# Local-attention stack on one core: spreading copies of one slot in eight on VectorE, the input's split two slots later, the first gate copy behind the squares of Q, and a rotary sum as one addition

## The chip, the cores and the metric

One NeuronCore of a Trainium2 chip runs the whole program. The metric is the device time of one execution in microseconds (us). Engines: TensorE (PE in the profile, its weight loads PEld), VectorE (DVE), ScalarE (ACT), GpSimd (POOL), and the DMA queues, which SyncE (SP) fills. Each engine works its own list of instructions in order; they meet only through semaphores.

## The reference

`x` is 8 x 256 x 128. After one layer norm without gains, two branches are computed and added to `x`: a causal attention (16 heads of 64, keys and values through a latent of 128), and a stack of 6 layers. A layer is

```python
def attn_layer(x, Wqkv, qs, ksc, Wo):
    q, k, v = split(x @ Wqkv)                     # 16 heads of 64
    q, k = l2norm(q) * qs, l2norm(k) * ksc
    q = q * cos * scale + rotate_half(q) * sin * scale
    k = k * cos / scale + rotate_half(k) * sin / scale
    return local_attention(q, k, v) @ Wo          # windows of 32 and the window before
def ffn_layer(x, g, bln, W1, b1, W2, b2):
    xn = layernorm(x) * g + bln
    a, gate = split(xn @ W1 + b1)                 # 341 each
    return a * gelu(gate) @ W2 + b2
for i in range(6):
    x = attn_layer(shift_tokens(x), ...) + x
    x = ffn_layer(shift_tokens(x), ...) + x
```

`rotate_half` puts minus the second half of a head's 64 features before the first half. All is float32.

## The kernel before, in words

**Stages.** The layer norm and the causal attention come first (to about 340 us). Then a stream of 192 slots does the six layers. A *unit* is one batch element of one layer (48 of them), a *group* is 4 of its 16 heads, and slot `s` is the step in which group `s` has its window scores computed. At the same time slot `s` works on other groups at other stages: it projects K, Q and V of group `s+4` (`keys`, `queries`, `values`, lines 1020 to 1040, three matmuls to a product of float32r halves), norms group `s+3` (L975, L703, L706), weighs the values of group `s-1` (L1016), projects the output of group `s-2` (L943), and does the MLP of two units, spread over slots 13 to 20 of a pair (`mlp_slot(s, k)` is true where `s` is `k` modulo 8). The pattern repeats every 8 slots. Below, **slot kind k** is a slot whose number is k modulo 8. In kinds 5, 6, 7 the gate's three products are done (L1077, copied out by L730), in kinds 1, 2, 3 the three of the other half (L1091, multiplied with the gate by `hidden_out`, L1373), in kind 4 the down projection (L1099). In kind 2 and kind 6 the centring matmul of the layer norm (L1113) follows, in the same PSUM bank `B_M` as the MLP, and in kinds 3 and 7 its variance (L1121).

**Order.** It is written out by hand: every engine has a function `slot(s)` that lists what it does in the slot.

- TensorE (lines 1042 to 1121): turn the probabilities of `s-1` (L1004), scores of `s` (L994), K, output projection, norms (L975), values (L1016), the MLP's product, Q, V, and last the centring (L1113) or variance (L1121). L1016 waits for `spread_ready`. L994 waits for `mask_laid`; only in kind 1 does TensorE lay the mask itself (L985). L1113 waits in kind 2 for `hid_ready` of the slot's own `hidden_out`, since it writes the bank which that reads.
- VectorE (lines 1393 to 1429): residual of the MLP, `shift_windows` (L1309, L1311), rotation of K (L1330, L1331), `weigh_down` (L1316 to L1321), the clamp of the norms (L1410), `residual` in kinds 1 and 5, `split_input` in kinds 0 and 4 (L1335 casts a unit's input to float32r, L1337 subtracts to get the rest), `hidden_out`, and last the rotation of Q, which waits for `q_square`.
- ScalarE (lines 682 to 745): `spread_out(s-1)` (L638 twice: the turned probabilities go from PSUM bank `B_T` to `spread`, two halves of 64 partitions), the exponentials (L699), logarithm and exponential of the norms (L703, L706), output copy (L670), squares of K (L629), gate copy (L730) in kinds 5, 6, 7, `lay_masks(s+1)` (L663), squares of Q (L629 again), the copy of the values (L569). `lay_masks` waits for `weights_ready` (L1321). At the end of kind 0 comes the **gelu session**: a table load (L674), two gelus (L676, L680), and at the start of kind 1, behind `spread_out`, the load back (L694).
- GpSimd (lines 442 to 470): the rotary sum of K (`rotated`, L439, two additions of 128x256), its norming (L432, released by L1410), the sum of squares (L459), norming of Q, the rotary sum of Q. In four slots of each of the five changes of layer it also splits the next weights (L420, L427). `rotate` on VectorE waits for the rotary sum before (`k_summed`, `q_summed`).
- SyncE: the copies of z and of shifted values for the windows, and the weights.

Of the kernel before, what the change touches and what calls it, by code (L numbers as in the profile page):

```python
# [11 lines left out]
ALU = mybir.AluOpType  # L12
ACT = mybir.ActivationFunctionType
# [4 lines left out]
NB, T = 8, 256  # L18
# [3 lines left out]
G, HG = 4, 4  # L22
# [3 lines left out]
WIN = 32  # L26
LN_EXP = "natural_log_exp_and_others"
INNER = P * 4 * 2 // 3
CW = [P, P, INNER - 2 * P]
# [11 lines left out]
KEYS = 2 * WIN  # L41
TILES = P // WIN

UNITS = DEPTH * NB
GROUPS = UNITS * G
LAYER = NB * G
# [55 lines left out]
def build(nc, x, w_kv_down, w_kv_up, w_q, w_out, Wqkv, q_scale, k_scale, Wo, ln_g, ln_b, W1, b1, W2, b2, const, out):  # L102
    with ExitStack() as ctx:
# [101 lines left out]
        def after(eng, name, value):  # L205

            if not (isinstance(value, int) and value <= 0):
                eng.wait_ge(S[name], value)
# [38 lines left out]
        def active(s, first, last):  # L247

            return first <= s < last

        def mlp_slot(s, first):

            return s % (2 * G) == first % (2 * G) and first <= s < first + 2 * G * MLPS
# [152 lines left out]
        def _(pool):  # L406
# [27 lines left out]
            def rotated(m, parity, idx, prod, mark):  # L434

                pool.wait_ge(S[prod], m + 1)
                after(pool, "zn_ready", m - 1)
                for half in range(2):
                    a = pool.tensor_tensor(z_raw[:, parity, idx, half, :], rot_u[:, idx, half, :], rot_v[:, idx, 1 - half, :], ALU.add)  # L439
                a.then_inc(S[mark], 1)  # L440

            def slot(s):
                one, two = active(s, -4, GROUPS - 4), active(s, -3, GROUPS - 3)
# [76 lines left out]
        def _(act):  # L520
# [105 lines left out]
            def squares(m, done, src, idx, mark):  # L626
                act.wait_ge(S[done], m + 1)
                after(act, "sums_ready", m)
                act.activation(sq[:, idx, :, :], src[:, :].rearrange("p (a t) -> p a t", a=2), ACT.Square).then_inc(S[mark], 1)  # L629
# [35 lines left out]
            def output_out(n):  # L665
# [3 lines left out]
                after(act, "lwo_done", n + 1 - G)  # L669
                act.activation(yt[:, 2 * og:2 * og + 2, :], B_T.rearrange("p (c t) -> p c t", c=2), ACT.Copy).then_inc(S["lyt_ready"], 1)  # L670

            def gelus(p):

                act.preload_act_table(ACT.Gelu)  # L674
                act.wait_ge(S["gate_ready"], 3 * p + 3)
                act.activation(gate[:, 0:2, :], gate[:, 0:2, :], ACT.Gelu).then_inc(S["gelu_done"], 1)  # L676
# [5 lines left out]
            def slot(s):  # L682
                g = s % G
                one, two = active(s, -4, GROUPS - 4), active(s, -3, GROUPS - 3)
                three, four = active(s, 0, GROUPS), active(s, 1, GROUPS + 1)
                normed = g == 0 and active(s, 2 * G, 2 * G + GROUPS)
                if two and s >= 0 and not mlp_slot(s, 17):
                    values_out(s + 3)
                if s == 1:
                    act.wait_ge(S["spread_zero"], 2)  # L690
                if four:
                    spread_out(s - 1)
                if mlp_slot(s, 17):
                    act.preload_act_table_set(LN_EXP)  # L694
                if normed:
                    deviations((s - 8) // G, B_M)
                if three:
                    act.wait_ge(S["shifted"], s + 1)
                    act.activation(both, both, ACT.Exp).then_inc(S["raised"], 1)  # L699
                if two:  # L700
                    m = s + 3
                    act.wait_ge(S["n_done"], m + 1)
                    act.activation(ln_n(m), B_N[:, :].rearrange("p (a t) -> p a t", a=2), ACT.Ln, bias=tiny[:, 0:1], scale=LNS).then_inc(S["ln_done"], 1)  # L703
                    act.wait_ge(S["ln_done"], m + 1)
                    after(act, "zn_ready", m)
                    act.activation(rinv(m), ln_n(m), ACT.Exp, scale=-0.5).then_inc(S["rinv_ready"], 1)  # L706
                if four:
                    output_out(s - 1)
                if one:
                    squares(s + 4, "k_prod", B_K, 1, "k_square")  # L710
                l = layer_begun(s, LAYER - 5)
                if l:
                    rotary_scales(l)
                    rotary_tables(l, 1)
                l = layer_begun(s, LAYER - 4)
                if l:
                    act.wait_ge(S["q_prod"], LAYER * l)
                    rotary_tables(l, 0)
                if g == 3 and active(s, 7, 7 + GROUPS):
                    xc_squares((s - 7) // G)  # L720
                if normed and s % (2 * G) == G:
                    gained((s - 8) // G)
                if s % (2 * G) == 1 and active(s, 9, 9 + GROUPS):
                    gained((s - 9) // G)
                for c in range(3):
                    if mlp_slot(s, 13 + c):
                        p = (s - 13 - c) // (2 * G)
                        act.wait_ge(S["gate_done"], 3 * p + c + 1)
                        after(act, "hid_ready", 3 * p + c - 2)
                        act.activation(gate[0:CW[c], c, :], B_M[0:CW[c], :], ACT.Identity, bias=gate_bias[0:CW[c], c:c + 1]).then_inc(S["gate_ready"], 1)  # L730
                if active(s, 0, GROUPS - 1) and lays_mask(s + 1):
                    lay_masks(s + 1)
                if one:
                    squares(s + 4, "lq_done", B_Q, 0, "q_square")
                if mlp_slot(s, 16):
                    if active(s + 1, -3, GROUPS - 3):
                        values_out(s + 4)
                    gelus((s - 16) // (2 * G))
                    last_gelus((s - 16) // (2 * G))
                l = layer_begun(s, LAYER + 6)  # L740
                if l:
                    gains(l)
                l = layer_begun(s, LAYER + 10)
                if l:
                    gate_biases(l)
# [470 lines left out]
        def _(dve):  # L1216
# [86 lines left out]
            def by_block(a):  # L1303
                return a[:, :, :].rearrange("p (a b) x -> p a (b x)", a=2)

            def shift_windows(n):

                dve.wait_ge(S["scores_done"], n + 1)
                dve.tensor_reduce(by_block(nm), both, AX_X, ALU.max, negate=True).then_inc(S["top_ready"], 1)  # L1309
                dve.wait_ge(S["top_ready"], n + 1)  # L1310
                dve.tensor_tensor(both, both, by_block(nm).unsqueeze(3).broadcast_to([P, 2, 4, KEYS]), ALU.add).then_inc(S["shifted"], 1)  # L1311
# [81 lines left out]
            def slot(s):  # L1393
                g = s % G
                one, two, three = active(s, -4, GROUPS - 4), active(s, -3, GROUPS - 3), active(s, 0, GROUPS)
                if mlp_slot(s, 21):
                    mlp_residual((s - 21) // (2 * G), B_M)
                if g == 3 and active(s, 7, 7 + GROUPS):
                    centred_out((s - 7) // G)
                if three:  # L1400
                    shift_windows(s)
                if one:
                    rotate(s + 4, 1, B_K, "lk_done", "k_summed", "k_prod")
                if g == 0 and active(s, 8, 8 + GROUPS):
                    normed_out((s - 8) // G)
                if three:
                    weigh_down(s)
                if two:
                    dve.wait_ge(S["rinv_ready"], s + 4)
                    dve.tensor_scalar(rinv(s + 3), rinv(s + 3), 1e12 / ROOT, None, ALU.min).then_inc(S["bound_ready"], 1)  # L1410
                if s == 0:
                    dve.wait_ge(S["wo_done"], NB + 1)
                    dve.tensor_copy(attn[:, NB - 1, :], B_Y[:, 0:T]).then_inc(S["res_done"], 1)
                if g == 1 and active(s, 5, 5 + GROUPS):
                    residual((s - 5) // G)
                if g == 0 and active(s, -4, GROUPS - 8):
                    unit = (s + 8) // G
                    after(dve, "lv_done", G * (unit - 1))
                    after(dve, "mlp_res", (s + 8 - LAYER) // (2 * G) + 1)
                    split_input(unit, (s + 8) // G % NB, (s + 8) // G % 2)  # L1420
                for c in range(3):
                    if mlp_slot(s, 17 + c):
                        p = (s - 17 - c) // (2 * G)
                        hidden_out(p, c, B_M, 2 * p + (2 if c == 2 else 1))
                if one:
                    rotate(s + 4, 0, B_Q, "q_square", "q_summed", "q_prod")
                l = layer_begun(s, LAYER + 15)
                if l:
                    out_biases(l)
# [93 lines left out]
```

## Time and profile before

| | |
|---|---|
| median of 3 runs | 1923.13 us (1921.1 to 1923.8) |
| profiled execution | 1922.0 us, its span 1920.2 us |
| TensorE, VectorE, ScalarE, GpSimd busy | 94%, 82%, 77%, 72% of the span |
| granted TensorE clock | 0.999 of full speed |
| one turn of 8 slots in the stream | 64.75 us (the one from 988.86 us on); 68.99 us where a layer changes |

The profile is of one execution. A duration in a timeline is that of one instruction from start to end; instructions of one engine overlap by about 0.1 us, so the distance of two starts is shorter. An idle time in brackets stands with the engine's next instruction and names whose signal ended it.

### The profile page before, as it was taken

Reading aid. Unit: us, or ns where it says so; the run is one execution under the profiler, and the core shown is the slowest. Engines: PE = TensorE matmul, PEld = TensorE weight load, DVE = VectorE, ACT = ScalarE, POOL = GpSimd, SP = SyncE. Lnnn points to the kernel's source line nnn. Section 1 sums busy time; section 2 is a strip of 40 time slices with the busy share of each in tenths; the row PEclk is TensorE's granted clock in tenths of the full one; section 3 lists DMA queues with packets and bytes.
Section 4 is the critical chain, followed back from the end, with each engine's and each line's share of the span. In section 5 each row is a group of like instructions: output and inputs, shape, how many; then the busy total and the mean of one; then the engine's idle time right before and its main releaser. Section 6 shows DMA issues by size and latency. Waiting matters only on the chain.

```text
span 1920.2 us, 68296 instructions
## 1 busy us (share of the span) xinstructions
PE 1813.2 (94%) x26763; PEld 1373.4 (72%) x26763; DVE 1572.1 (82%) x3052; ACT 1480.1 (77%) x3020; POOL 1374.0 (72%) x1455
## 2 busy tenths in 40 slices
PE   6999998999989999999999899999999998999997
PEld 4777765777767777777777677777777776777774
DVE  5776777888888888888888888888888888888886
ACT  5766665688778878887887788788878887887885
POOL 3010024898898787897888987878978889888880
PEclk9999999999999999999999999999999999999999
DMA  4000001344434334333334343343333443433332
GB/s 133 1 1 0 0 0 37 98 107 107 129 88 108 101 99 129 91 96 102 101 101 127 86 110 99 99 134 90 96 100 99 105 128 83 112 96 100 100 98 71
DMA packets 193540, 171.03 MB, mean 89 GB/s; under 512 B 32304, under 2 KB 190168, under 8 KB 193240
## 3 DMA queue, kind: packets, MB, share of 16 engines
q1 hardware_dynamic: 193240, 166.89, 33.1%
q8 instruction: 206, 3.38, 0.8%
q14 instruction: 94, 0.77, 0.1%
HBM read 21.01 MB, written 1.05 MB: 11 GB/s over the span
## 4 chain that ended last, share of the span: by engine, by line
PE 59%; ACT 18%; DVE 11%; issue 9%; SPq 1%; POOL 1%; DMA 0%; ACTq 0%; DVEq 0%; POOLq 0%
PE bank L975 6%; PE bank L1016 6%; PE bank L943 5%; PE pair_bank L994 5%; PE bank L1025 4%; ACT probs L703 3%; ACT sq L629 3%; PE bank L1027 3%; PE bank L1026 3%; PE bank L1077 2%; PE bank L1099 2%; ACT yt L670 2%; PE bank L1004 2%; PE bank L860 2%; PE bank L1091 2%
## 5 line engine op out<-in xcount | busy, mean ns | idle before, releaser
L439 POOL TENSOR_TENSOR z_raw<-rot_u,rot_v 128x256 f32<-128x256 f32 x768 | 552.7, 744 | 70.4 <-DVE rot_v L1331 67.8
L432 POOL TENSOR_TENSOR z_norm<-probs_t,z_raw 128x512 f32<-128x512 f32 x376 | 480.8, 1279 | 119.6 <-DVE probs_t L1410 117.4
L1330 DVE TENSOR_TENSOR rot_u<-bank,tabs 128x512 f32<-128x512 f32 x384 | 263.0, 685 | 160.0 <-ACT sq L629 159.8
L1025 PE MATMUL bank<-x_high,w_high 128*128 128x256 f32 x768 | 301.7, 393 | 0.2 <-issue 0.2
L459 POOL TENSOR_TENSOR sqs<-sq 128x512 f32<-128x512 f32 x192 | 250.5, 1305 | 71.0 <-issue 70.9
L1016 PEld LDWEIGHTS bank<-probs_t,v_late 128*64 128x64 f32 x3072 | 157.6, 137 | 160.1 <-issue 160.1
L1331 DVE TENSOR_TENSOR rot_v<-bank,tabs 128x512 f32<-128x512 f32 x384 | 261.3, 680 | 0.0
L699 ACT ACTIVATE pair_bank<-pair_bank 128x512 f32<-128x512 f32 x192 | 111.7, 582 | 190.7 <-DVE pair_bank L1311 189.7
L638 ACT ACTIVATE probs_t<-bank 64x512 f32<-64x512 f32 x384 | 226.5, 590 | 24.6 <-PE bank L1004 22.1
L629 ACT ACTIVATE sq<-bank 128x512 f32<-128x512 f32 x384 | 224.9, 594 | 26.6 <-PE bank L1027 20.4
L1027 PE MATMUL bank<-x_low,w_high 128*128 128x256 f32 x768 | 216.4, 282 | 0.0
L1026 PE MATMUL bank<-x_high,w_low 128*128 128x256 f32 x768 | 216.3, 282 | 0.0
L1016 PE MATMUL bank<-probs_t,v_late 128*64 128x64 f32 x3072 | 198.8, 228 | 15.3 <-ACT probs_t L638 15.3
L975 PE MATMUL bank<-sqs,consts 128*128 128x512 f32 x384 | 197.5, 596 | 6.0 <-POOL sqs L459 5.8
L943 PE MATMUL bank<-yt,wo 128*128 128x256 f32 x768 | 197.8, 380 | 0.0
L994 PE MATMUL pair_bank<-zqk 64*32 64x64 f32 (+1 forms) x12288 | 164.9, 221 | 30.2 <-ACT pair_bank L663 29.6
L1016 PE MATMUL bank<-probs_t,v_sb 128*64 128x64 f32 x3072 | 190.2, 222 | 0.0
L1025 PEld LDWEIGHTS bank<-x_high,w_high 128*128 128x128 f32 x768 | 144.8, 189 | 58.5 <-issue 39.0
L994 PEld LDWEIGHTS pair_bank<-zqk 64*32 64x32 f32 x12288 | 134.9, 105 | 65.8 <-issue 64.2
L1026 PEld LDWEIGHTS bank<-x_high,w_low 128*128 128x128 f32 x768 | 145.5, 189 | 36.9 <-issue 36.9
L703 ACT ACTIVATE probs<-bank,tiny 128x512 f32<-128x512 f32 x188 | 129.2, 687 | 45.4 <-PE bank L975 43.1
L1016 PEld LDWEIGHTS bank<-probs_t,v_sb 128*64 128x64 f32 x3072 | 158.6, 138 | 0.0
(184 smaller groups left out, 4525.5 us busy)
## 6 DMA issues: line engine op xcount, KB each, us to landing
zqk<-z_norm SPq DMA_DIRECT2D x1536, 64.0 KB, 2.1
v_late<-v_sb SPq DMA_DIRECT2D x192, 192.0 KB, 2.6
w_qkv<-in_L_ffn_Wqkv SPq DMA_DIRECT2D x18, 512.0 KB
v_late<-v_sb SPq DMA_DIRECT2D x192, 32.0 KB, 3.0
wo<-in_L_ffn_Wo SPq DMA_DIRECT2D x24, 128.0 KB, 2.4
w<-in_L_ffn_W SPq DMA_DIRECT2D x12, 170.5 KB, 2.6
z_norm<-in_L_attn_x SPq DMA_DIRECT2D x4, 256.0 KB, 5.1
w_qkv<-in_L_attn_w_kv_up SPq DMA_DIRECT2D x4, 256.0 KB, 4.5
```

The costliest lines, as they stand in the source:

```text
L432: return pool.tensor_tensor(z_norm[:, parity, idx, :, :], rinv(m)[:, idx, :].unsqueeze(1).broadcast_to([P, 2, T]), z_raw[:, parity, idx, : ...
L439: a = pool.tensor_tensor(z_raw[:, parity, idx, half, :], rot_u[:, idx, half, :], rot_v[:, idx, 1 - half, :], ALU.add)
L629: act.activation(sq[:, idx, :, :], src[:, :].rearrange("p (a t) -> p a t", a=2), ACT.Square).then_inc(S[mark], 1)
L943: mm = pe.matmul(B_X[:, 0:T], wo[:, c, :], yt[:, c, :], start=(c == 0), stop=(c == HD // P - 1))
L975: pe.matmul(B_N[:, :], con("blk"), sqs[:, :, :].rearrange("p a t -> p (a t)"), start=True, stop=True).then_inc(S["n_done"], 1)
L994: mm = pe.matmul(bank[a][WIN * tile:WIN * tile + WIN, at + skip:at + KEYS], zqk[rows, g, 0, pair, WIN * j:WIN * j + WIN], zqk[rows, g, 1, ...
L1016: mm = pe.matmul(y[:, t, tile % 2, :, :], (v_sb if tile % 2 else v_late)[:, odd, t, f], spread[:, h, tile, :], start=True, stop=True, tile ...
L1025: pe.matmul(dst, w_high[:, j, cols], x_high[:, odd, :], start=True, stop=False)
L1026: pe.matmul(dst, w_low[:, j, cols], x_high[:, odd, :], start=False, stop=False)
L1027: mm = pe.matmul(dst, w_high[:, j, cols], x_low[:, odd, :], start=False, stop=True)
L1330: dve.tensor_tensor(rot_u[:, idx, :, :], src, tabs[:, 2 * idx, :, :], ALU.mult)
L1331: dve.tensor_tensor(rot_v[:, idx, :, :], src, tabs[:, 2 * idx + 1, :, :], ALU.mult).then_inc(S[mark], 1)
```

## The change

1. In the 22 slots of kind 1 from slot 17 on, `spread_out(s-1)` is VectorE's first step, as two copies, and no longer ScalarE's: there the load back (L694) follows the gelus.
2. `split_input` of a unit stands in kinds 2 and 6, two slots later, with the same waits; in VectorE's list it stays ahead of `hidden_out` and of the rotation of Q.
3. The gate copy of kind 5 (c = 0) stands behind `lay_masks` and the squares of Q; those of kinds 6 and 7 stay.
4. `rotated` on GpSimd is one addition of 128x512 with `rot_v` read in reversed order of its halves, in place of two of 128x256.

```diff
@@ GpSimd, rotated @@
-                for half in range(2):
-                    a = pool.tensor_tensor(z_raw[:, parity, idx, half, :], rot_u[:, idx, half, :], rot_v[:, idx, 1 - half, :], ALU.add)
-                a.then_inc(S[mark], 1)
+                pool.tensor_tensor(z_raw[:, parity, idx, :, :], rot_u[:, idx, :, :], rot_v[:, idx, ::-1, :], ALU.add).then_inc(S[mark], 1)
@@ ScalarE, slot @@
-                if four:
+                if four and not mlp_slot(s, 17):
                     spread_out(s - 1)
                 if mlp_slot(s, 17):
                     act.preload_act_table_set(LN_EXP)
...
-                for c in range(3):
+                for c in (1, 2):
                     if mlp_slot(s, 13 + c):
...
+                        gate_out((s - 13 - c) // (2 * G), c)
                 if active(s, 0, GROUPS - 1) and lays_mask(s + 1):
                     lay_masks(s + 1)
                 if one:
                     squares(s + 4, "lq_done", B_Q, 0, "q_square")
+                if mlp_slot(s, 13):
+                    gate_out((s - 13) // (2 * G), 0)
@@ VectorE @@
+            def spread_out(n):
+
+                dve.wait_ge(S["turned"], n + 1)
+                after(dve, "lpv_done", n)
+                tiles = B_T.rearrange("p (h s c) -> p h s c", h=HG, s=TILES)
+                for x in range(2):
+                    rows = slice(KEYS * x, KEYS * x + KEYS)
+                    a = dve.tensor_copy(spread[rows, :, :, WIN * x:WIN * x + WIN], tiles[rows, :, :, :])
+                a.then_inc(S["spread_ready"], 1)
@@ VectorE, slot @@
+                if mlp_slot(s, 17) and active(s, 1, GROUPS + 1):
+                    spread_out(s - 1)
                 if mlp_slot(s, 21):
                     mlp_residual((s - 21) // (2 * G), B_M)
...
-                if g == 0 and active(s, -4, GROUPS - 8):
-                    unit = (s + 8) // G
+                if g == 2 and active(s, -2, GROUPS - 6):
+                    unit = (s + 6) // G
                     after(dve, "lv_done", G * (unit - 1))
-                    after(dve, "mlp_res", (s + 8 - LAYER) // (2 * G) + 1)
-                    split_input(unit, (s + 8) // G % NB, (s + 8) // G % 2)
+                    after(dve, "mlp_res", (s + 6 - LAYER) // (2 * G) + 1)
+                    split_input(unit, unit % NB, unit % 2)
                 for c in range(3):
                     if mlp_slot(s, 17 + c):
```

`gate_out` on ScalarE holds the three lines of the gate copy that stood in the loop (wait for `gate_done`, wait for `hid_ready`, the activation of L730).

## Rows read from the trace of the kernel before

**Rows 1.** Waits: engine and line waiting, releaser: us in total, times, longest
```profile
PE pair_bank L994 <- ACT pair_bank L663: 29.6, 46, 0.8
...
PE bank L1016 <- ACT probs_t L638: 15.3, 23, 0.7
...
PE bank L975 <- POOL sqs L459: 5.8, 7, 1.0
```

**Rows 2.** ScalarE's timeline, gelu session (kinds 0 and 1): start, us, instruction
```profile
991.12 0.61 ACT L680 ACTIVATE gate<-gate 85x512 f32<-85x512 f32 x1
991.64 1.18 ACT L638 ACTIVATE probs_t<-bank 64x512 f32<-64x512 f32 x2
992.83 1.28 ACT L694 ACT_TABLE_LOAD   x1
...
997.43 0.60 ACT L663 ACTIVATE pair_bank<-mask_local_b 128x512 f32<-128x512 bf16 x1
```

**Rows 3.** TensorE's timeline, kinds 1 and 2
```profile
992.96 0.34 PE L1016 MATMUL bank<-probs_t,v_late 128*64 128x64 f32 x4 [0.66 <-ACT probs_t L638]
...
998.18 0.84 PE L994 MATMUL pair_bank<-zqk 64*32 64x32 f32 x64 [0.84 <-ACT pair_bank L663]
...
1005.09 0.67 PE L1113 MATMUL bank<-xs,consts 128*128 128x256 f32 x2
```

**Rows 4.** VectorE's timeline, kinds 1 and 2
```profile
990.91 0.68 DVE L1309 TENSOR_REDUCE nm<-pair_bank 128x8 f32<-128x512 f32 x1
...
998.58 0.69 DVE L1330 TENSOR_TENSOR rot_u<-bank,tabs 128x512 f32<-128x512 f32 x1 [0.30 <-ACT sq L629]
...
1004.20 0.74 DVE L1373 SCALAR_TENSOR_TENSOR hid<-bank,out_bias,gate 128x512 f32<-128x512 f32 x1
```

**Rows 5.** VectorE's timeline, end of kind 0, a turn later
```profile
1052.68 0.29 DVE L1335 CAST x_high<-xs 128x256 fp32r<-128x256 f32 x1
1053.01 1.40 DVE L1337 TENSOR_TENSOR x_low<-xs,x_high 128x256 fp32r<-128x256 f32 x1
1054.33 0.68 DVE L1330 TENSOR_TENSOR rot_u<-bank,tabs 128x512 f32<-128x512 f32 x1
```

**Rows 6.** ScalarE (squares of K and Q) and GpSimd beside rows 5
```profile
1052.02 1.07 ACT L629 ACTIVATE sq<-bank 128x512 f32<-128x512 f32 x2
...
1052.85 1.28 POOL L432 TENSOR_TENSOR z_norm<-probs_t,z_raw 128x512 f32<-128x512 f32 x1 [0.69 <-DVE probs_t L1410]
```

**Rows 7.** Lines L1337 and L1299: ns min/median/max, first and last start
```profile
L1337 DVE TENSOR_TENSOR x_low<-xs,x_high x48: 426/1394/1403, 284.6 to 1809.9; 128x256 fp32r<-128x256 f32 x48
...
L1299 DVE COPY zqk<-bank x32: 678/681/692, 17.2 to 280.5; 128x512 f32<-128x512 f32 x32
```

**Rows 8.** ScalarE's timeline, kind 5
```profile
1029.69 0.69 ACT L730 ACTIVATE gate<-bank,gate_bias 128x512 f32<-128x512 f32 x1
1030.26 0.61 ACT L663 ACTIVATE pair_bank<-mask_local_b 128x512 f32<-128x512 bf16 x1
```

**Rows 9.** VectorE and TensorE beside rows 8
```profile
1029.09 0.69 DVE L1321 TENSOR_TENSOR probs<-pair_bank,rrec 128x512 f32<-128x512 f32 x1 [0.23 <-DVE rrec L1318]
...
1031.02 0.84 PE L994 MATMUL pair_bank<-zqk 64*32 64x32 f32 x64 [0.46 <-ACT pair_bank L663]
```

**Rows 10.** A change of layer, kind 2 on VectorE and kind 6 on TensorE
```profile
541.84 1.67 DVE L1410 TENSOR_SCALAR probs_t<-probs_t 128x512 f32<-128x512 f32 x1
...
572.06 0.84 PE L994 MATMUL pair_bank<-zqk 64*32 64x32 f32 x64 [0.63 <-ACT pair_bank L663]
```

**Rows 11.** The page's groups of GpSimd: busy us, mean ns of one, idle before
```profile
L439 POOL TENSOR_TENSOR z_raw<-rot_u,rot_v 128x256 f32<-128x256 f32 x768 | 552.7, 744 | 70.4 <-DVE rot_v L1331 67.8
...
L459 POOL TENSOR_TENSOR sqs<-sq 128x512 f32<-128x512 f32 x192 | 250.5, 1305 | 71.0 <-issue 70.9
```

**Rows 12.** VectorE's timeline, a split's cast at the stream's start, and a rotation in kind 6
```profile
344.17 1.26 DVE L1335 CAST x_high<-xs 128x256 fp32r<-128x256 f32 x1
...
1038.62 0.69 DVE L1330 TENSOR_TENSOR rot_u<-bank,tabs 128x512 f32<-128x512 f32 x1 [1.49 <-ACT sq L629]
```

More of the change, by code:

```diff
@@ L670, in output_out, with gate_out @@
                 act.activation(yt[:, 2 * og:2 * og + 2, :], B_T.rearrange("p (c t) -> p c t", c=2), ACT.Copy).then_inc(S["lyt_ready"], 1)
+            def gate_out(p, c):
+                act.wait_ge(S["gate_done"], 3 * p + c + 1)
+                after(act, "hid_ready", 3 * p + c - 2)
+                act.activation(gate[0:CW[c], c, :], B_M[0:CW[c], :], ACT.Identity, bias=gate_bias[0:CW[c], c:c + 1]).then_inc(S["gate_ready"], 1)
             def gelus(p):
@@ L724, in slot @@
                     gained((s - 9) // G)
-                for c in range(3):
+                for c in (1, 2):
                     if mlp_slot(s, 13 + c):
[L727 to L730, printed above, removed]
+                        gate_out((s - 13 - c) // (2 * G), c)
                 if active(s, 0, GROUPS - 1) and lays_mask(s + 1):
```

## The prediction

> **What bounds the kernel now.** The table first: TensorE is busy for 94% of the span at a granted clock of 0.999, the other engines for 72 to 82%. In the stream the time is TensorE's list plus the stretches in which it stands still, so I read the waits for those [rows 1]. Two belong to this change: L1016 stands for ScalarE's spreading copies 23 times (15.3 us), and L994 for the mask that ScalarE lays 46 times (29.6 us). The timelines say where. In kind 1, behind the gelu session, L1016 idles 0.66 us and the next slot's L994 0.84 us [rows 3]; in kind 5 the next slot's L994 idles 0.46 us [rows 9]. The same values come back in turn after turn. What stands behind them on ScalarE: the last gelu, two copies, the table load, and then without a pause the rest of the slot up to the mask at 997.43 [rows 2]. VectorE matters where it hands over to this list: its rotation of Q in kind 1 waits 0.30 us for ScalarE's squares, and from there it works without a gap to `hidden_out` of kind 2 at 1004.20 [rows 4]. That step is the one to keep in view: L1113 begins at 1005.09 [rows 3], 0.89 us behind the start of L1373, whose 0.74 us it must await. TensorE arrives there at that very moment, so this is a second limit, touching and hidden.
>
> **Part 1, the spreading copies (22 slots).** The load back begins 0.02 us after the last gelu's end, 991.12 + 0.61 = 991.73, so at 991.75, in place of 992.83 [rows 2]: ScalarE's list from there to the mask and the squares of Q comes 1.08 us earlier. On VectorE two copies are added. The nearest row is the copy of 128x512 from PSUM, 0.68 us [rows 7]; two are 1.2 us if the second overlaps the first, as a rotation's two halves do by 0.1 us, and 1.4 us if it does not, which I take. They have room: with the split gone from kind 0 the rotation of Q before them begins when the squares are there, at 1052.02 + 1.07 = 1053.09 [rows 6] in place of 1054.33 [rows 5], 1.2 us earlier. L1309 at 990.91 [rows 4] then begins at about 991.1 with the copies in front, L1311 is done at 992.5, and ScalarE needs that only after its load, 991.75 + 1.28 = 993.03. Slack 0.5 us. If that cover were gone, each further tenth on VectorE would cost a tenth. L1016 starts at once; its 0.66 us are part of the gain, not on top, because L994 still awaits the mask. The mask comes at 996.35 and L994 at 997.10. Gain 1.08 us x 22 = 23.8 us.
>
> **Part 2, the split two slots on.** A split costs 1054.33 - 1052.68 = 1.65 us of VectorE's list [rows 5]. Leaving kind 0 makes the room of part 1. Leaving kind 4 gives nothing: the rotation of Q there waits for TensorE's long slot anyway. In kind 6 it falls into a wait of VectorE for the squares, 1.49 us [rows 12]; the 0.16 us over are hidden behind TensorE. In kind 2 it stands ahead of `hidden_out`, with L1113 right behind. In the new positions L1373 starts at 1004.20 - 1.08 + 1.65 = 1004.77, and L1113 0.89 us later, 1005.66, against 1005.09. So the gain of part 1 turns into a loss of 0.57 us by the end of kind 2: the split costs 1.65 us of TensorE's time there. The queue behind L1113 is all of slot kind 3, and nothing in it catches up, as TensorE is the bound there. This happens in 21 slots (18 to 178), 16 in ordinary turns and 5 in changes of layer: 16 x 1.65 = 26.4 us.
>
> Why 1.65 and not the sum of its own times: L1337 takes 1.39 us in the median, but 0.43 us at its fastest [rows 7]. In the row it starts at 1053.01 beside a GpSimd product that ends at 1054.13 [rows 6], and ends 0.28 us behind that. The clamp L1410 releases this product, and in kind 2 the clamp again stands right before the split, so the same collision comes along. The lower bound is 0.29 + 0.43 with overlap, 0.67 us; the upper is the slowest cast, 1.26 us at the stream's start [rows 12], with 1.39 us for the subtraction, 2.65 us. I take 1.65, since the neighbours in kind 2 are those of kind 0. The Trainium skill, GPSIMD Engine Reference, section 8 (Key points), says that GpSimd shares its SBUF interfaces with VectorE, with contention for two-port instructions and those with two SBUF inputs; by that rule L1337, with two SBUF inputs, queues in kind 2 too, and the trace agrees with its 0.43 against 1.39 us. Without the rule the split would be the lower bound, 0.67 us, the first rival below.
>
> **Part 3, the gate copy of kind 5 (22 or 23 slots).** It stands ahead of the mask for 1030.26 - 1029.69 = 0.57 us [rows 8]. But the mask also waits for L1321, which ends at 1029.09 + 0.69 = 1029.78 [rows 9]; so it starts at 1029.81, 0.45 us earlier, and L994's idle 0.46 us closes. The copy itself moves to about 1030.8; TensorE wants its bank in the next slot only. 17 ordinary slots x 0.45 = 7.7 us; in the 5 changes of layer the idle time is 0.63 us [rows 10], of which 0.57 goes: 2.9 us. Together 10.6.
>
> **Part 4, the rotary sum.** Two additions take 2 x 0.744 us, one of the double width is a sum like L459, 1.305 us [rows 11]: 0.18 us less, 384 times. In ordinary turns GpSimd waits for VectorE's clamp, so this is nothing; were the reversed reading as slow as twice 0.744, that would be nothing either, as 0.7 us idle stand before its product [rows 6]. In the changes of layer GpSimd splits weights and has no slack: L975 stands for its sum of squares, 5.8 us in 7 waits, some 0.96 us in each change [rows 1]. Eight sums of 0.18 make 1.4 us, so these go: 4.8 us.
>
> **Changes of layer, kind 2.** There the clamp already takes 1.67 us beside GpSimd's work [rows 10]. A split behind it meets two GpSimd instructions in a row, the sum of double width and the product: 1.28 + 1.28 and a tail of 0.2, about 2.7 us. 5 x 2.7 = 13.5 us.
>
> **The sum.** Costs 26.4 + 13.5 = 39.9; gains 23.8 + 10.6 + 4.8 = 39.2. About 0.5 us more comes back at the start, where the slow split [rows 12] leaves slot 0. So 1922.0 us of the profiled execution become 1922.2. The median of the runs is 1.1 above that execution, within their spread, so I forecast 1922.5 us: no change. A measurement of this kernel can tell about 0.2%, 3.8 us.
>
> **Rivals.**
> 1. *The split finds its way free in kind 2* (faster). For it: the sums of part 4 end earlier, so GpSimd's state differs a little. Against: 1.39 us is the median of 48. Then L1113 would come at 1004.68 or so, 0.4 us early in place of 0.57 late: 16 x 1.0 = 16 us, and twice that per change of layer, 10: 1896 us. Chance 0.12. Between it and the forecast (split 1.3 us, or the load back by the full 1.19 us earlier that the two copies span): 7 us, 1915. Chance 0.15.
> 2. *Both halves of the split queue behind GpSimd* (slower). Place: kind 2, between the clamp and L1373. Price: 2.65 - 1.65 = 1.0 us per turn, 16 times, 16 us: 1938. It decides from the point where the product L432 starts before the cast L1335 has been taken; now the cast comes first by 0.17 us [rows 5, 6]. Chance 0.13.
> 3. *ScalarE's gain in kind 5 is taken by the next wait* (slower): L994 follows the sequence of L1004, and part 3 gives little. 10 us, 1932. Chance 0.10.
>
> **Numbers.** Forecast 0.50, rivals as said. Faster 0.27, same 0.50, slower 0.23. The range goes from 1901 (leaving out the end of rival 1, 0.12) to 1940 (rival 2 within).
>
> **What the profile would show.** Right: L1016's waits for spreading copies gone from kind 1; L694 right behind L680; L994's wait in kind 1 still there, near 0.5 us; L994's wait in kind 5 gone; a new wait of L1113 on L1373 of about 1.6 us in 16 turns and more in 5; L975's waits on L459 gone in the changes of layer; L1337 at 1.4 us in kinds 2 and 6. Turns of about 64.9 us. Wrong: no wait at L1113 (rival 1), L1335 above 0.8 us in kind 2 (rival 2), or ScalarE waiting for L1311 behind its table load.

## The result, and the profile after

| | before | changed |
|---|---|---|
| median | 1923.28 us (6 runs, 1921.1 to 1926.4) | 1929.11 us (6 runs, 1924.9 to 1931.5) |
| ratio | | 1.0026 (95% interval 1.0016 to 1.0037) |
| profiled execution, its span | 1922.0, 1920.2 us | 1924.88, 1923.1 us |
| mean granted TensorE clock of the runs | 0.998 to 1.000 (the 53 later runs of this kernel) | 0.992 to 0.996 |

The changed kernel is slower by 0.26%, just outside what I called no change. I had forecast 1922.5 us and no change. The profiled execution is the fastest of the six; it is 2.9 us over that of before in span. Line numbers have moved: L1019 is L1016 of before, L997 is L994, L1116 is L1113, L1386 is L1373 (`hidden_out`), L1348 and L1350 are the split, L1425 the clamp, L978 is L975, L1124 is L1121.

The waits of the changed kernel, engine and line waiting, releaser, us in total, times, longest:

```profile
PE bank L1116 <- DVE hid L1386: 42.6, 21, 3.7
...
PE pair_bank L997 <- ACT pair_bank L661: 15.8, 23, 0.7
...
PE bank L978 <- POOL sqs L457: 3.3, 6, 0.6
```

Against [rows 1]: L1016's wait for spreading copies is gone (0.5 us in the tail of the stream is left), L994's has halved (kind 5 is gone, kind 1 stays), and L1116's 42.6 us in 21 waits are new. An ordinary turn on ScalarE (start, us, instruction), to be laid beside [rows 2]:

```profile
991.64 0.61 ACT L684 ACTIVATE gate<-gate 85x512 f32<-85x512 f32 x1
992.27 1.28 ACT L698 ACT_TABLE_LOAD   x1
...
996.76 0.60 ACT L661 ACTIVATE pair_bank<-mask_local_b 128x512 f32<-128x512 bf16 x1
```

On VectorE, beside [rows 4, 5]:

```profile
990.10 1.38 DVE L1316 COPY probs_t<-bank 64x512 f32<-64x512 f32 x2
991.51 0.69 DVE L1322 TENSOR_REDUCE nm<-pair_bank 128x8 f32<-128x512 f32 x1
...
1003.52 0.29 DVE L1348 CAST x_high<-xs 128x256 fp32r<-128x256 f32 x1
1003.84 1.41 DVE L1350 TENSOR_TENSOR x_low<-xs,x_high 128x256 fp32r<-128x256 f32 x1
1005.17 0.74 DVE L1386 SCALAR_TENSOR_TENSOR hid<-bank,out_bias,gate 128x512 f32<-128x512 f32 x1
```

On TensorE, beside [rows 3]:

```profile
997.50 0.92 PE L997 MATMUL pair_bank<-zqk 64*32 64x32 f32 x64 [0.72 <-ACT pair_bank L661]
...
1006.06 0.67 PE L1116 MATMUL bank<-xs,consts 128*128 128x256 f32 x2 [1.43 <-DVE hid L1386]
```

The load now starts 0.02 us after the last gelu, the two copies on VectorE take 1.38 us, the split stands ahead of `hidden_out` and its subtraction takes 1.41 us again, and TensorE's centring matmul waits for `hidden_out`. L1116 starts 0.89 us behind L1386. Step by step this is the ordinary turn of the prediction.

The turns as stretches (first an ordinary one, then two with a change of layer). The columns are length, busy time and count of PE, PEld, DVE, ACT, POOL, then the granted clock, DMA share and GB/s:

```profile
461.91:526.53 64.62, 62.37 (x1031) 47.76 (x1037) 55.97 (x100) 51.62 (x92) 50.70 (x41) 1.00 0.45 121
526.53:596.99 70.46, 64.29 (x1031) 48.70 (x1037) 60.15 (x100) 54.69 (x103) 61.26 (x49) 0.98 0.35 90
...
790.94:860.13 69.19, 62.97 (x1031) 47.78 (x1036) 60.55 (x100) 54.70 (x102) 61.24 (x49) 1.00 0.35 89
```

And the same change of layer before:

```profile
526.83:595.82 68.99, 63.43 (x1031) 47.74 (x1035) 58.92 (x98) 55.96 (x104) 63.91 (x65) 1.00 0.35 91
```

Over the whole trace, 16 ordinary turns went from 64.77 to 64.64 us in the mean (2.1 us less), the five changes of layer from 345.1 to 351.5 us in sum (6.4 us more), and the last stretch of slots from 53.5 to 52.4 us. So the loss is in the changes of layer, and there it comes with the clock: the four turns at a lower clock (70.46, 70.62, 70.46 and 70.76 us) are together 5.5 us longer than four of 69.19, while the whole execution is 2.9 us longer than before. The change at 526.53, VectorE first, with GpSimd beside it:

```profile
540.33 1.54 DVE L1425 TENSOR_SCALAR probs_t<-probs_t 128x512 f32<-128x512 f32 x1
541.80 1.35 DVE L1348 CAST x_high<-xs 128x256 fp32r<-128x256 f32 x1
543.18 1.36 DVE L1350 TENSOR_TENSOR x_low<-xs,x_high 128x256 fp32r<-128x256 f32 x1
```

```profile
541.55 1.44 POOL L438 TENSOR_TENSOR z_raw<-rot_u,rot_v 128x512 f32<-128x512 f32 x1
542.96 1.31 POOL L432 TENSOR_TENSOR z_norm<-probs_t,z_raw 128x512 f32<-128x512 f32 x1
```

The cast ends some 0.15 us behind the one GpSimd instruction (543.15 and 542.99), the subtraction some 0.28 us behind the next (544.54 and 544.27). Then TensorE, and stretches of 3 us around it:

```profile
545.35 1.19 PE L1116 MATMUL bank<-xs,consts 128*128 128x256 f32 x2 [3.68 <-DVE hid L1386]
546.34 1.06 PE L1007 MATMUL bank<-consts,probs 128*128 128x128 f32 x4
```

```profile
540.00:543.00 3.00, 1.67 (x13) 1.38 (x11) 3.00 (x3) 2.24 (x5) 3.00 (x3) 1.00 0.43 107
543.00:546.00 3.00, 0.65 (x2) 0.59 (x3) 2.97 (x5) 0.00 (x0) 3.00 (x3) 0.85 0.46 123
546.00:549.00 3.00, 3.00 (x74) 2.31 (x73) 1.30 (x3) 1.18 (x2) 2.92 (x4) 0.58 0.13 32
549.00:552.00 3.00, 3.00 (x41) 2.14 (x40) 2.90 (x6) 1.37 (x3) 2.56 (x2) 1.00 0.35 82
```

TensorE stands for 3.68 us, and when it goes on the granted clock is at its lower level for some 3 us (1.2 of 2.4 GHz, mean 0.58 over 3 us); L1116's pair takes 1.19 in place of 0.67 us. In the change at 790.94 the stall is the same 3.68 us, no stretch around it is below 1.00, and the turn is 1.3 us shorter.

### The profile page after: what moved, and what is told of

Same layout as the page of the kernel before. It is cut to its first block, busy times and chain, and to the rows that moved or that the text cites. A ratio compares the mean times of both kernels' runs of the same rounds, so it can differ in the third digit from the quotient of the medians.

```text
span 1923.1 us, 67912 instructions
## 1 busy us (share of the span) xinstructions
PE 1810.2 (94%) x26763; PEld 1373.9 (71%) x26763; DVE 1599.5 (83%) x3096; ACT 1455.4 (76%) x2976; POOL 1317.4 (69%) x1071
## 4 chain that ended last, share of the span: by engine, by line
PE 62%; ACT 14%; DVE 9%; issue 8%; SPq 4%; POOL 2%; DMA 0%; ACTq 0%; DVEq 0%; POOLq 0%
PE bank L978 6%; PE bank L946 6%; PE bank L1019 6%; PE pair_bank L997 5%; PE bank L1028 4%; SPq L358 3%; PE bank L1080 3%; PE bank L1007 3%; PE bank L1029 3%; PE bank L1030 3%; PE bank L1102 2%; ACT sq L627 2%; PE bank L863 2%; ACT probs L707 2%; ACT yt L668 2%
## 5 line engine op out<-in xcount | busy, mean ns | idle before, releaser
L438 POOL TENSOR_TENSOR z_raw<-rot_u,rot_v 128x512 f32<-128x512 f32 x384 | 496.2, 1296 | 122.1 <-DVE rot_v L1344 119.8
L1019 PEld LDWEIGHTS bank<-probs_t,v_late 128*64 128x64 f32 x3072 | 155.1, 137 | 144.4 <-issue 144.4
L636 ACT ACTIVATE probs_t<-bank 64x512 f32<-64x512 f32 x340 | 200.9, 591 | 65.5 <-PE bank L1007 63.3
L978 PE MATMUL bank<-sqs,consts 128*128 128x512 f32 x384 | 197.1, 595 | 3.4 <-POOL sqs L457 3.3
L1019 PE MATMUL bank<-probs_t,v_late 128*64 128x64 f32 x3072 | 198.9, 228 | 0.5 <-ACT probs_t L636 0.5
L1019 PE MATMUL bank<-probs_t,v_sb 128*64 128x64 f32 x3072 | 189.6, 222 | 0.0
L997 PE MATMUL pair_bank<-zqk 64*32 64x64 f32 (+1 forms) x12288 | 163.5, 222 | 17.1 <-ACT pair_bank L661 15.8
L997 PEld LDWEIGHTS pair_bank<-zqk 64*32 64x32 f32 x12288 | 133.0, 106 | 52.2 <-issue 50.7
L707 ACT ACTIVATE probs<-bank,tiny 128x512 f32<-128x512 f32 x188 | 129.2, 687 | 42.6 <-PE bank L978 40.5
L1019 PEld LDWEIGHTS bank<-probs_t,v_sb 128*64 128x64 f32 x3072 | 156.1, 138 | 0.0
```

Source lines behind the costliest of these rows:

```text
L438: pool.tensor_tensor(z_raw[:, parity, idx, :, :], rot_u[:, idx, :, :], rot_v[:, idx, ::-1, :], ALU.add).then_inc(S[mark], 1)
L978: pe.matmul(B_N[:, :], con("blk"), sqs[:, :, :].rearrange("p a t -> p (a t)"), start=True, stop=True).then_inc(S["n_done"], 1)
L997: mm = pe.matmul(bank[a][WIN * tile:WIN * tile + WIN, at + skip:at + KEYS], zqk[rows, g, 0, pair, WIN * j:WIN * j + WIN], zqk[rows, g, 1, ...
L1019: mm = pe.matmul(y[:, t, tile % 2, :, :], (v_sb if tile % 2 else v_late)[:, odd, t, f], spread[:, h, tile, :], start=True, stop=True, tile ...
```

## Experiments

All are timed against the kernel before (medians 1923.3 to 1924.5 us in the three groups). Two theories are set against each other. Theory C: the waits and gains cancel as predicted, and the fall of the clock behind the long stall is what comes on top. Theory W: the clock plays no part.

### The changed kernel again

No edit.

> The changed kernel once more, for a second trace. Theory C (clock): the waits of L1116 (L1113 before) on hidden_out cancel the gains, as predicted, and what comes on top are falls of TensorE's granted clock behind the 3.7 us stall where a layer changes. Then runs between 1924 and 1932 us order by their mean clock (0.996 to 0.992), and in a slower run's trace the falls are in all five changes of layer and longer (3 us and more each at about half clock), while ordinary turns stay at 64.6 us. Theory W (waits): the clock has nothing to do with it; a slower run then has longer or more waits than the first trace, and its changes of layer at full clock take longer than 69.2 us. Either way the median is 1927 to 1931 us.

Measured: 1929.61 us, ratio 1.0036 (1.0024 to 1.0048). Its trace has ordinary turns of 64.69 us in the mean and changes of layer of 70.49, 70.67, 70.44, 70.73 and 71.87 us, all five at a mean clock of 0.98 or 0.95, with stalls of 3.66 to 3.69 us each: as long as those of the first trace, where one kept the clock and took 69.19. Over the twelve runs of both, time and mean clock go together (1924.9 us at 0.996, 1932.8 at 0.991). A line through them has a slope of 1.26 us per 0.001 and gives 1922 us at 0.999; it is a coarse figure, since the mean clocks are known to 0.001 only. The first trace gives another: without the 5.5 us of its four turns its span is 1917.6 us, 2.6 us below the kernel before. By either, nothing is lost at the clock of before. That speaks for C, and against W: stalls of one length go with turns of two lengths, and the longer ones have the lower clock.

### The split alone, and the copies alone

The split's new place on the kernel before; then VectorE's `spread_out` on the kernel before:

```diff
-                if g == 0 and active(s, -4, GROUPS - 8):
-                    unit = (s + 8) // G
+                if g == 2 and active(s, -2, GROUPS - 6):
+                    unit = (s + 6) // G
```

```diff
-                if four:
+                if four and not mlp_slot(s, 17):
                     spread_out(s - 1)
+                if mlp_slot(s, 17) and active(s, 1, GROUPS + 1):
+                    spread_out(s - 1)
```

(The last two lines stand at the head of VectorE's slot.)

> The kernel before with only the split moved (kinds 2 and 6, ahead of hidden_out). Without the spreading copies on VectorE nothing makes ScalarE earlier, so by the prediction's step L1113 comes 1.65 us later in 16 ordinary turns, 26 us; in changes of layer the stall adds 2.6 us and, by theory C, 1.3 to 2.8 us of clock fall: 1923 + 26 + 5 x 4.5 = 1971 us, wait of L1113 on hidden_out 16 x 1.6 + 5 x 3.7 = 44 us. Rival: the split leaves kind 0, where it delayed the rotation of Q by 1.2 us, and this comes back as an earlier kind 1: then some 10 us less, 1960 us.

Measured: 1960.13 us, ratio 1.0185 (1.0171 to 1.0199). Ordinary turns 66.43 us in the mean, 1.66 us over before: the price of part 2, which was put at 1.65. The 11 us missing from my 1971 are in the changes of layer: the stall is 2.7 us there, not 3.7, and the turns take 69.96 (clock 1.00) to 72.68 us, in sum 11.5 us over before where I had set 22. In this kernel the rotary sum is two additions, and the cast and the subtraction take 0.81 and 0.83 us beside them (in place of 1.35 and 1.36). The rival was nearer in time, but not by its reason: nothing came back in kind 1.

```profile
PE bank L1113 <- DVE hid L1373: 37.8, 21, 2.7
```

> The kernel before with only the spreading copies of kind 1 on VectorE (split stays in kinds 0 and 4). VectorE has no room: its two copies (1.4 us) put L1311 at 992.3 + 1.4 = 993.7 against the load's end at 993.03, so ScalarE's first exponential comes 0.4 us earlier in place of 1.08: 22 x 0.4 = 9 us off, 1914 us, with ScalarE waiting for L1311 behind the load. Rival: the spreading copies overlap and cost 1.2 us: 0.6 us x 22 = 13 us, 1910 us. If the prediction's price of part 1 were wrong altogether (no gain without the split's move), 1923 us.

Measured: 1911.07 us, ratio 0.9934 (0.9921 to 0.9948), 13 us off. Ordinary turns 64.35 us, 0.42 us less, which is the 0.4 that VectorE's lack of room leaves (ScalarE idles 0.75 us for L1324, L1311 of before, behind its load); the changes of layer give 0.6 us each and the last stretch 1.4. A new wait says what is short:

```profile
PE bank L1007 <- DVE probs L1334: 12.0, 25, 1.0
```

TensorE now waits 0.48 us in each turn, at the start of kind 2, for VectorE's probabilities of kind 1. So part 1 alone was a gain of 0.7%, and the whole change spends it.

### hidden_out ahead of the split

```diff
-                if g == 2 and active(s, -2, GROUPS - 6):
...
-                    split_input(unit, unit % NB, unit % 2)
                 for c in range(3):
                     if mlp_slot(s, 17 + c):
                         p = (s - 17 - c) // (2 * G)
                         hidden_out(p, c, B_M, 2 * p + (2 if c == 2 else 1))
+                if g == 2 and active(s, -2, GROUPS - 6):
...
+                    split_input(unit, unit % NB, unit % 2)
```

> The changed kernel with hidden_out ahead of the split in kind 2. Both theories: the wait of TensorE's centring matmul on hidden_out (42.6 us in 21 waits) falls to the five short ones of before (about 1.1 us each). Theory C: ordinary turns 64.6 - 1.5 = 63.1 us, changes of layer 70.5 - 2.6 - 1.3 = 66.6 us with the granted clock back at 0.999 of full speed; together 16 x 1.5 + 5 x 4 = 44 us off, 1885 us. Theory W: same waits gone but no clock effect, 16 x 1.5 + 5 x 2.6 = 37 us off, 1892 us, mean clock unchanged at about 0.993. Rival H (the split is a cost wherever it stands in kind 2, since it delays the rotation of Q and the next slot's scores): a new wait of at least 1 us takes its place on TensorE in kind 3, and the time stays above 1910 us.

Measured: 1904.27 us, ratio 0.9905 (0.989 to 0.9919), clock 0.997 to 0.999. Both theories had it faster. The wait at L1116 is gone from ordinary turns, but they only fell to 64.09 us, not 63.1, because another took its place. That is rival H in its main point, a new wait in kind 3; its bounds (1 us, 1910 us) were too high, the new wait is 0.8 us:

```profile
PE bank L1124 <- DVE hid L1386: 12.9, 16, 0.8
...
PE bank L1124 <- ACT xc L656: 10.4, 6, 2.0
```

VectorE's timeline of kinds 2 and 3 shows why:

```profile
996.09 0.75 DVE L1386 SCALAR_TENSOR_TENSOR hid<-bank,out_bias,gate 128x512 f32<-128x512 f32 x1
996.75 0.94 DVE L1348 CAST x_high<-xs 128x256 fp32r<-128x256 f32 x1
997.73 1.38 DVE L1350 TENSOR_TENSOR x_low<-xs,x_high 128x256 fp32r<-128x256 f32 x1
...
1004.97 0.74 DVE L1386 SCALAR_TENSOR_TENSOR hid<-bank,out_bias,gate 85x512 f32<-85x512 f32 x1
```

0.7 us later the split meets two GpSimd instructions instead of one: 2.3 us in place of 1.65, near the 2.65 of my second rival, in another place. VectorE is then late for the `hidden_out` of kind 3, for which the variance matmul L1124 waits. The limit from kind 1 to kind 3 is VectorE, and a reordering inside it moves the wait on.

### The reordering in changes of layer only, and in ordinary turns only

The edit of the last section, the place chosen by `s % LAYER == LAYER - 6`, and by its opposite.

> hidden_out ahead of the split only in the slot of kind 2 in which a layer changes (5 slots), the 16 others as in the changed kernel. Theory C: the stall there falls from 3.7 to about 1.1 us, no fall of the clock is left, mean clock 0.999; changes of layer from 70.5 to about 66.6 us: 1929 - 20 = 1909 us, and the spread of the runs is as narrow as before the change. Theory W: 5 x 2.6 = 13 us off, 1916 us, clock still below 0.997. If the falls came from the 1.5 us stalls of ordinary turns, the clock would stay at 0.993.

> The counterpart: hidden_out ahead of the split in the 16 ordinary slots of kind 2, the five in changes of layer as in the changed kernel. Theory C: 16 x 1.5 = 24 us off, 1905 us; the 3.7 us stalls and the falls of the clock stay, mean clock 0.992 to 0.996 and changes of layer of 69.2 or 70.5 us. Theory W: also about 1905 us, but with changes of layer that do not tell two lengths apart by the clock.

Measured: 1917.23 us, ratio 0.9972 (0.9963 to 0.998), and 1919.65 us, ratio 0.9981 (0.9973 to 0.999). In the first, the stall of 3.7 us is gone from the changes of layer (1.0 us at L1116, then 2.0 at L1124, where `xc` of ScalarE is awaited), but in its trace four of five still have a lower clock: 68.5 us, and 67.34 in the one without; its runs have mean clocks of 0.993 to 0.996. My figure of 0.999 was wrong, and the spread of the runs is not narrow either (8.5 us). In `hidden_first`, with these same two waits, the trace shows one fall in five. What differs between the two kernels are the ordinary turns around (1.5 us of waiting in kind 2, or 0.8 in kind 3); that this is the reason is not shown. The falls follow the second stall: L1124 starts at 813.51 us there, and the stretches around it are

```profile
809.00:812.00 3.00, 2.57 (x19) 1.80 (x14) 2.93 (x6) 2.94 (x8) 2.92 (x4) 1.00 0.36 86
812.00:815.00 3.00, 1.49 (x5) 1.21 (x6) 1.16 (x2) 2.94 (x7) 2.75 (x3) 0.78 0.39 99
815.00:818.00 3.00, 3.00 (x75) 2.45 (x74) 2.17 (x5) 2.07 (x4) 3.00 (x3) 0.65 0.27 75
...
1895.30:1899.50 4.20, 4.15 (x7) 2.11 (x8) 2.57 (x5) 2.46 (x4) 0.00 (x0) 0.59 0.19 62
```

The last line is a sixth place, behind the stream's end, with two waits of 0.96 us close together. In the second kernel, all five changes of layer are at 0.98 and take 70.5 to 70.6 us; ordinary turns take 64.08 us there, 64.68 in the first, and have a clock of 1.00 in both. So the falls in the stream belong to the changes of layer, a stall of 3.7 us is not the only thing that brings them, and 1.5 us in ordinary turns never did in any trace. Outside the stream's turns there are three more over all the traces: the one above, one at 1940.4 us in the trace of the split alone, and one at 334.3 us, ahead of the stream, in that of the sum alone.

### The rotary sum as two additions

```diff
-                pool.tensor_tensor(z_raw[:, parity, idx, :, :], rot_u[:, idx, :, :], rot_v[:, idx, ::-1, :], ALU.add).then_inc(S[mark], 1)
+                for half in range(2):
+                    a = pool.tensor_tensor(z_raw[:, parity, idx, half, :], rot_u[:, idx, half, :], rot_v[:, idx, 1 - half, :], ALU.add)
+                a.then_inc(S[mark], 1)
```

on the changed kernel, and the reverse of it on the kernel before:

> The changed kernel with the rotary sum as two additions again. In changes of layer the cast of the split waits for the GpSimd instruction in flight; with halves it waits for 0.7 us in place of 1.3, so the stall of TensorE in kind 2 falls from 3.7 to about 3.1 us. GpSimd itself is 0.18 us slower per sum, so the wait for its sum of squares in kind 6 grows by up to 1.4 us. Theory C: the clock still falls (stall of 3 us), time 1929 + 5 x (0.8 - 0.6) = 1930 us. If a stall of 3.1 us is short enough for the clock to hold, 1923 us and mean clock 0.999.

> The kernel before with only the rotary sum as one addition. Prediction's part 4: nothing in ordinary turns, L975's wait of 0.96 us gone in five changes of layer, 1918 us. Theory P (the longer instruction holds the SBUF path, and the clamp and casts of VectorE wait for it in changes of layer): the gain there is 0.4 us or less, 1921 to 1923 us; with the whole changed kernel, undoing this part made the changes of layer at full clock 68.8 in place of 69.2 us.

Measured: 1926.02 us, ratio 1.0004 (0.9995 to 1.0013), and 1920.34 us, ratio 0.9982 (0.9973 to 0.9991). In the first, the stall at `hidden_out` in changes of layer is 2.7 us, 1.0 less:

```profile
PE bank L1118 <- DVE hid L1388: 37.9, 21, 2.7
```

The cast takes 0.81 and the subtraction 0.83 us, each beside one addition of the halves and again ending 0.15 and 0.28 us behind it. So both do wait for the end of the GpSimd instruction in flight. Without a fall the turn takes 68.76 us against 69.19; four of five falls stay, and mean clocks are 0.994 to 0.999. In the second, changes of layer take 68.43 in place of 69.03 us, 3 us in all; my 4.8 was high, since 0.45 us of a new wait for VectorE's probabilities appears in them. Ordinary turns, said to stay, became 0.07 us longer with 0.12 us of the same wait. The one addition is a gain on its own and a loss where the split's cast stands behind it.

### The gate copy alone

The third part of the change on the kernel before.

> The kernel before with only the gate copy of kind 5 behind the mask and the squares of Q. By the prediction's part 3 the wait of L994 in kind 5 (0.46 us, 0.63 where a layer changes) goes and nothing takes its place: 10.6 us off, 1913 us, ordinary turns 64.3 us. Rival (the next wait takes it): 1923 us.

Measured: 1914.93 us, ratio 0.9954 (0.9941 to 0.9968). Ordinary turns 64.28 us: 0.49 less, as in part 3. Changes of layer stay at 69.0:

```profile
PE bank L980 <- POOL sqs L459: 8.0, 6, 1.5
```

L975's wait (L980 here) grew from 0.96 to 1.5 us there. GpSimd is the limit, so what part 3 gives in a change of layer is taken by the next wait; my 2.9 us for it needed part 4.

### The split in kinds 3 and 7, behind hidden_out

```diff
+                if g == 3 and active(s, -1, GROUPS - 5):
+                    unit = (s + 5) // G
+                    after(dve, "lv_done", G * (unit - 1))
+                    after(dve, "mlp_res", (s + 5 - LAYER) // (2 * G) + 1)
+                    split_input(unit, unit % NB, unit % 2)
```

in place of the changed kernel's, behind the loop over `hidden_out`.

> The changed kernel with the split another slot later (kinds 3 and 7) and behind hidden_out. By theory V (VectorE is the limit from kind 1 to kind 3, and TensorE feels it at each hidden_out; behind the last of them the split is hidden): no wait of TensorE on hidden_out in ordinary turns, kind 3's 0.8 us that appeared with hidden_out first gone too, turns of 63.2 us: 16 x 0.85 = 14 us less than the 1904 us of that kernel, 1890 us. In changes of layer the waits stay at about 1.1 and 1.2 us, no clock fall, 66.5 us. Rival: K of kind 4 needs x_split at once, and a new wait on TensorE of about 0.8 us takes the place: 1904 us.

Measured: 1883.15 us, ratio 0.9787 (0.9774 to 0.9801), clock 0.998 to 1.000: faster than both kernels, 40 us below the one before. Ordinary turns 63.07 us with one wait of TensorE left (0.73 us for the mask), changes of layer 66.8 to 67.0, no fall of the clock in the trace. There the split takes 1.1 us, not 1.65:

```profile
997.23 0.75 DVE L1386 SCALAR_TENSOR_TENSOR hid<-bank,out_bias,gate 85x512 f32<-85x512 f32 x1
997.90 0.76 DVE L1348 CAST x_high<-xs 128x256 fp32r<-128x256 f32 x1
998.70 0.42 DVE L1350 TENSOR_TENSOR x_low<-xs,x_high 128x256 fp32r<-128x256 f32 x1
```

> split_in_three with the rotary sum as two additions. Where the split does not stand behind the clamp of kind 2, the length of GpSimd's instruction should matter little: within 3 us of 1883 us. Theory P says the two additions are not slower, 1881 to 1883 us; the prediction's part 4 says 5 x 0.96 us slower in changes of layer, 1888 us.

With two additions on top, ratio to the kernel before as always: 1886.87 us, ratio 0.9818 (0.9801 to 0.9834). The changes of layer take 67.8 in place of 66.9 us, 0.9 each, which is what the prediction's part 4 says; here theory P, by which the two additions are not slower, is wrong.

### The mask of kind 1 ahead of the gain

On the kernel with the split in kinds 3 and 7, `lay_masks` of kind 1 moved ahead of `gained` on ScalarE.

> split_in_three with the mask of kind 1 laid ahead of the layer norm's gain (L652 before) on ScalarE. The only regular wait of TensorE left is L997 (L994 before) for that mask, 0.7 us in kind 1. The gain takes 0.49 us of ScalarE's list, so the wait falls to 0.2 us: 22 x 0.49 = 11 us off 1883, 1872 us. Rival: VectorE's rotation of Q is the limit in kinds 1 to 2 and the turn keeps its 63.05 us because hidden_out of kind 2 becomes the wait: then 1883 us with a new wait at L1116 of up to 0.5 us.

Measured: 1884.44 us, ratio 0.979 (0.9776 to 0.9804), no different from 1883.15. The rival of the expectation holds, and the turn keeps its 63.1 us:

```profile
PE bank L1118 <- DVE hid L1388: 12.4, 22, 1.4
...
PE pair_bank L999 <- ACT pair_bank L661: 4.8, 22, 0.2
```

The wait for the mask is down to 0.2 us, and in ordinary turns the centring waits 0.3 us for `hidden_out` instead.

## Why the prediction was wrong

**Right, and shown.** What bounds the kernel, and the hidden second limit at L1113. Part 1: load behind the gelus without a pause, copies 1.38 us (1.4 taken), VectorE's cover wide enough; alone 0.42 us per turn, as its missing cover makes it. Part 2: 1.65 us per ordinary turn, 1.66 measured alone. The wait at L1116: 1.5 us (1.6 said). Ordinary turns were said to grow by 0.12 us and shrank by 0.13. Part 3 in ordinary turns: 0.45 said, 0.49 measured.

**Right by its place, mis-sized.** Part 4 in changes of layer: the wait of L975 did not go, it fell from 0.96 to about 0.55 us (row L978 above, and [rows 1]), 2 us in place of 4.8. In the changed kernel part 4 is even a cost there: with two additions a change of layer at full clock takes 68.76 us, with one 69.19. The prediction had its lengthening of the split within the 2.7 us of that split, but not against part 4. The split in kind 2 there: 2.67 us (541.80 to 544.47), 2.7 said. At a full clock a change of layer was to stay as long as before, and took 69.19 against 69.03 us. And 1922.5 us leaves out the 1.1 us between the profiled execution and the median, which by the prediction's own sum would make 1923.3, no change either.

**The step that failed** is the sentence "So 1922.0 us of the profiled execution become 1922.2", in which every term was taken at the granted clock of before. The stall in changes of layer, 3.7 us, which is the prediction's own 2.7 us of split on the 1.1 us that stood there already, less 0.1, is followed by some 3 us at the lower clock: 1.3 to 1.6 us more in four of five turns of the first trace, 1.3 to 2.7 in all five of the second. Nothing of the kind was among the rivals. The median rose by 5.8 us. By the line through the twelve runs the changed kernel would be at 1922 us with the clock of before; that is a fit, not a run. By the first trace the falls cost 5.5 us, and its span without them is 2.6 us below before, where the sum said 0.2 above: the ordinary turns shrank by 0.13 us and were said to grow by 0.12, 4 us in 16 turns. So at full clock the sum was 2.8 us too high, and the falls turned a small gain into the loss that was measured.

**Rivals.** The first (a free way) did not happen in kind 2; a partly free one does in kind 3. The second (both halves queue) did not happen in ordinary turns, but did in the changes of layer and in kind 2 behind `hidden_out`. The third (the next wait takes part 3) holds in changes of layer only, and is seen there with the gate copy alone.

**Open.** Why one stall of 3.68 us in five let the clock stand (none did in the second trace), and why two kernels with the same waits in changes of layer fell once and four times in five. No run varied the stall alone. A kernel that adds only a stall was not tried, so that the stall brings the fall is argued from this: the seven traces in whose changes of layer TensorE stands for at most 1.7 us at once show no fall there, and the seven with stalls of 2.0 us and more show one to five each. Even so, two of the five runs of the split in kinds 3 and 7 with two additions (stalls of up to 1.7 us) have a mean clock of 0.997, at 1890.9 and 1891.9 us against 1885.4 to 1886.9 for the others.

## What to carry to other kernels

When a step moves on an engine that is not the bound, look for the instruction of the bound engine that stands nearest behind its new place, and compute how close it is now: here 0.00 us, so the whole step appeared on it, 1.65 us in 16 turns and 2.67 us in 5. A change of four parts can hide a good one: alone, the copies gave 0.7%, the gate copy 0.5% and the sum 0.2%, and moving the split one slot further, behind `hidden_out`, gave 2.1% in all. And where a sum contains a stall of several microseconds on TensorE, price the time after it at the lower clock as one of the cases.

## What the runs showed of the hardware that I had not expected

The fall of the granted clock behind stalls of 2.7 to 3.7 us, and in two kernels of 2.0 us: 0.58 in the mean of the 3 us that follow, and L1116's two matmuls at 1.19 in place of 0.67 us. The Trainium skill, TensorE: Matmul & The Clock Gate, Part 1, says that a gate passes fewer clock pulses to the array according to how busy it has been of late. The trace agrees with it in direction; that a stall of the same length leaves the clock at 1.00 in one change of layer and not in the others is what the traces add.

The cast and the subtraction of the split take 0.29 and 0.43 us where they start with GpSimd idle and up to 1.35 and 1.4 us where they do not. In the stream of every trace each such cast ends 0.15 us and each such subtraction 0.28 us behind the GpSimd instruction that was running when it began, whatever the length of that one: so making a GpSimd instruction longer costs VectorE, 1.0 us of stall in each change of layer here, while it makes GpSimd itself faster.
